# A perceiver layer on one core: opening zeros over all rows, the value bias in one product, output weights from slot 249, output projections four slots sooner, the last division behind the seam

## The reference, cut to what matters

```python
# cross-attention on the context, keys and queries rms-normed, masked by length
qh = rms_norm(q @ Wq, q_norm_w); kh = rms_norm(kv @ Wk, k_norm_w); vh = kv @ Wv
o = softmax(where(mask, qh @ kh.T / 8, NEG_INF)) @ vh
x = x + o @ Wo
# causal self-attention over 128 rows, with biases
qkv = einsum('bsd,dthe->bsthe', x, w_qkv) + b_qkv
x = x + einsum('bqhe,hed->bqd', softmax(q @ k.T / 8 - 1e9 * (1 - causal)) @ v, w_out) + b_out
# feed-forward, activations and weights rounded to fixed steps
x = x + act_qdq(act_qdq(gate * sig) * up) @ lpbq_dequant(w_down).T
```

## Time and profile before

| | |
|---|---|
| median of 3 runs | 1226.51 us |
| profiled execution, its time | 1228.04 us |
| its span | 1226.1 us |
| TensorE busy | 1161.4 us (95%) |
| VectorE | 814.8 us (66%) |
| ScalarE | 735.0 us (60%) |
| GpSimd | 874.3 us (71%) |
| transfers | 209.98 MB, queue q1 84.4% of 16 engines' span |
| cross-attention ends | about 967 us |
| self-attention | 971 to 1092 us |
| feed-forward | 1093 to 1226 us |

### The profile page before, as it was taken

One profiled execution on the slowest core, in us unless ns is written; L12 is line 12 of the kernel. 1 busy time (PEld: TensorE's weight loads), 2 busy tenths in 40 slices (PEclk: granted clock), 3 DMA queues, 4 the chain that ended last, 5 costly groups with the idle time before them and its releaser, 6 DMA issues. The chain is left out here.

```text
span 1226.1 us, 31362 instructions
## 1 busy us (share of the span) xinstructions
PE 1161.4 (95%) x11841; PEld 876.1 (71%) x11845; DVE 814.8 (66%) x1780; ACT 735.0 (60%) x1329; POOL 874.3 (71%) x750
## 2 busy tenths in 40 slices
PE   6899999999999999999999999999998899979958
PEld 4677777877888888788888878788885667534423
DVE  5778777697766678676666877666655444542772
ACT  5366655775767667666666776667666336512760
POOL 2689999888888898788888888898887423510510
PEclk9999999999999999999999999999999999989979
DMA  6579999999999999999999998999999533972000
GB/s 208 147 136 187 210 179 192 187 227 207 185 208 193 199 189 217 236 178 202 199 189 203 215 206 178 198 182 216 191 161 238 152 88 70 236 163 39 1 1 35
DMA packets 562345, 209.98 MB, mean 171 GB/s; under 512 B 506770, under 2 KB 529298, under 8 KB 562196
## 3 DMA queue, kind: packets, MB, share of 16 engines
q1 hardware_dynamic: 562196, 207.98, 84.4%
HBM read 66.27 MB, written 23.07 MB: 73 GB/s over the span
## 5 line engine op out<-in xcount | busy, mean ns | idle before, releaser
L144 PE MATMUL pair<-arena 128*128 128x256 f16 x2048 | 559.8, 273 | 15.6 <-DVE arena L655 7.8
L146 PE MATMUL pair<-arena 128*128 128x256 f16 x2048 | 558.9, 273 | 0.0
L145 PE MATMUL pair<-arena 128*128 128x256 f16 x2048 | 558.8, 273 | 0.0
L513 POOL TENSOR_TENSOR p_parts<-probs,p_parts 128x512 f16<-128x512 f32 x256 | 307.7, 1208 | 19.8 <-ACT p_parts L620 19.4
L523 POOL TENSOR_TENSOR k_rinv<-k_ms,half_neg 128x8 f32<-128x8 f32 x128 | 226.3, 1768 | 103.4 <-DVE k_ms L718 102.6
L144 PEld LDWEIGHTS pair<-arena 128*128 128x128 f16 x2048 | 200.2, 98 | 90.7 <-issue 47.7
L703 DVE CUSTOM_DVE_ANT_0 probs<-bank,mask 128x512 f32<-128x512 f32 x256 | 175.1, 684 | 114.8 <-PE bank L868 110.1
L620 ACT ACTIVATE p_parts<-probs 128x512 f16<-128x512 f32 x256 | 160.9, 629 | 100.7 <-DMA pt<-p_parts 89.2
L146 PEld LDWEIGHTS pair<-arena 128*128 128x128 f16 x2048 | 200.4, 98 | 23.7
L145 PEld LDWEIGHTS pair<-arena 128*128 128x128 f16 x2048 | 200.4, 98 | 20.8
L597 ACT ACTIVATE probs<-probs,neg_max 128x512 f32<-128x512 f32 x256 | 182.9, 714 | 8.7 <-DVE neg_max L712 8.7
(11 more groups left out here) (276 smaller groups left out, 1878.0 us busy)
## 6 DMA issues: line engine op xcount, KB each, us to landing
raws<-in_ctx_t_dram SPq DMA_DIRECT2D x64, 256.0 KB, 3.3
side_kept<-side_parts SPq DMA_DIRECT2D x40, 256.0 KB, 3.7
arena<-side_kept SPq DMA_DIRECT2D x40, 256.0 KB, 4.5
w_kept<-ffn_turned SPq DMA_DIRECT2D x36, 256.0 KB, 3.4
side_raw<-in_w_qkv_dram SPq DMA_DIRECT2D x24, 256.0 KB, 3.3
arena<-w_kept SPq DMA_DIRECT2D x24, 256.0 KB, 4.0
pt<-p_parts SPq DMA_TRANSPOSE x240, 3.7
ffn_raw<-in_w_gate_dram SPq DMA_DIRECT2D x12, 256.0 KB, 3.6
```

The costliest lines, as they stand in the source:

```text
L144: nc.tensor.matmul(to, x_hi[k], w_hi[k], start=(k == 0), stop=False)
L145: nc.tensor.matmul(to, x_hi[k], w_lo[k], start=False, stop=False)
L146: mm = nc.tensor.matmul(to, x_lo[k], w_hi[k], start=False, stop=(k == n - 1))
L513: nc.gpsimd.tensor_tensor(p_parts[n % PTS][:, 1, :], probs[n % PROBS][:, :], p_parts[n % PTS][:, 0, :], ALU.subtract).then_inc(p_lo_done, 1)
```

## The change

- `zeros` has 128 rows, and the opening product of a unit uses all of them.
- `OUT_FIRST, NORM_AT, WO_FIRST = (258, 262, 266), (262, 266), 249`: output projections and norms stand four slots sooner, and the two idle products of L876 stay in slot 257 alone. LAST is 274.
- The eight pieces of `Wo` are loaded one a slot from slot 249, each behind a wait for the projection that last reads its place in `ctx_lo`; the layout of `wo_at` changes so that a piece covers just two context tiles. The other 24 pieces keep two a slot, from slot 256.
- The last unit's division, split and transpose leave cross-attention and stand at the head of self-attention's lists. The second product of the ring (bank 7) waits for the division.
- The values' bias: one tile `bv_parts` holds the high part in all rows and the low part in rows 32 to 63; the weights `two_rows` are 1 in rows 0 and 32, zero elsewhere. One product of 128 rows takes the place of two of one row.

```diff
-OUT_FIRST, NORM_AT = (262, 266, 270), (266, 270)
+OUT_FIRST, NORM_AT, WO_FIRST = (258, 262, 266), (262, 266), 249
...
-        wo_at = arena[:, 24576:32768].rearrange("p (a k n) -> p a k n", a=2, k=GROUPS)
+        wo_at = arena[:, 24576:32768].rearrange("p (k a n) -> p a k n", a=2, k=GROUPS)
...
-        zeros = sb("zeros", [1, 2 * VW], F16, c)
+        zeros = sb("zeros", [P, 2 * VW], F16, c)
...
-        LAST = PARTS + PV_LAG + 4
+        LAST = PARTS + PV_LAG
...
-            return n // 8 if n is not None and n % 8 == 7 else None
+            return n // 8 if n is not None and n % 8 == 7 and n < PARTS - 1 else None
...
+                if 0 <= (j := slot - WO_FIRST) < GROUPS:
+                    if j == 0:
+                        for i in range(2):
+                            sp.wait_ge(side_kept_done[i], 16 * SIDES // 2)
+                    sp.wait_ge(proj_done, PARTS - GROUPS + 1 + j)
+                    sp.dma_start(side_home(j), side_kept[j].rearrange("p (a n) -> p a n", a=2)).then_inc(side_in[j // 4], 16)
                 if slot == PARTS:
                     sp.wait_ge(proj_done, PARTS)
...
-                for j in range(2 * (slot - PARTS), 2 * (slot - PARTS) + 2):
-                    if 0 <= j < DRAINED:
+                for j in range(GROUPS + 2 * (slot - PARTS), GROUPS + 2 * (slot - PARTS) + 2):
+                    if GROUPS <= j < DRAINED:
...
-                        nc.tensor.matmul(bank[7][:, 0:2 * VW], zeros[0:1, 0:P], zeros[0:1, :], start=True, stop=False)
+                        nc.tensor.matmul(bank[7][:, 0:2 * VW], zeros[:, 0:P], zeros[:, :], start=True, stop=False)
...
-                sp.dma_start(bv_row[i], g["b_qkv"][2 * E + D * i:2 * E + D * (i + 1)].partition_broadcast(1)).then_inc(bv_in, 16)
+                sp.dma_start(bv_row[i], g["b_qkv"][2 * E + D * i:2 * E + D * (i + 1)].partition_broadcast(P)).then_inc(bv_in, 16)
...
+            sp.wait_ge(last_lo_done, 1)
+            sp.dma_start_transpose(ot[:, B - 1, :, GROUPS - 1, :], last_parts[:, :, :].rearrange("p a n -> p (a n)")).then_inc(ot_in[1], 16)
             x_turned(0)
...
-            nc.gpsimd.memset(ones[:, :], 1.0).then_inc(ready, 1)
+            nc.gpsimd.memset(two_rows[:, :], 0.0).then_inc(zeroed, 1)
...
+            for i in range(2):
+                pool.wait_ge(zeroed, 3 + i)
+                nc.gpsimd.affine_select(out=two_rows[:, :], in_=two_rows[:, :], compare_op=ALU.not_equal, fill=1.0, base=-32 * i,
+                                        pattern=[[0, P]], channel_multiplier=1).then_inc(zeroed, 1)
...
+            pool.wait_ge(last_hi_done, 1)
+            nc.gpsimd.tensor_tensor(last_parts[:, 1, :], last_o[:, :, :].rearrange("p h e -> p (h e)"), last_parts[:, 0, :],
+                                    ALU.subtract).then_inc(last_lo_done, 1)
...
             def placed(key):
+                if at[key] == 1:
+                    pe.wait_ge(last_o_done, 1)
...
-                nc.tensor.matmul(to[:, :], ones[0:1, :], bv_hi[0:1, n * D:(n + 1) * D], start=True, stop=False)
-                nc.tensor.matmul(to[:, :], ones[0:1, :], bv_lo[0:1, n * D:(n + 1) * D], start=False, stop=False)
+                nc.tensor.matmul(to[:, :], two_rows[:, :], bv_parts[:, n * D:(n + 1) * D], start=True, stop=False)
...
+            nc.vector.reciprocal(last_rec[:, :], last_new[:, :, HD]).then_inc(last_rec_done, 1)
+            dve.wait_ge(last_rec_done, 1)
+            nc.vector.tensor_tensor(last_o[:, :, :], last_new[:, :, 0:HD], last_rec[:, :].unsqueeze(2).to_broadcast([P, 2, HD]),
+                                    ALU.mult).then_inc(last_o_done, 1)
```

More of the change, by code:

```diff
@@ L129, in program @@
             o_parts = [sb(f"o_parts{i}", [P, 2, P], F16, attn) for i in range(2)]
+            o_rec = [sb(f"o_rec{i}", [P, 2], F32, attn) for i in range(2)]
+            o_n = [sb(f"o_n{i}", [P, 2, HD], F32, attn) for i in range(2)]
             row_parts = [sb(f"row_parts{i}", [P, 2, D], F16, attn) for i in range(2)]
@@ L157, in cross_attention @@
             g[n] for n in ("resid", "ot", "xt", "wo_at", "w_qkv_at", "side_kept", "side_in", "ot_in", "xt_in", "o_parts", "bqk"))
-        o_rec = [sb(f"o_rec{i}", [P, 2], F32, c) for i in range(2)]
-        o_n = [sb(f"o_n{i}", [P, 2, HD], F32, c) for i in range(2)]
+        o_rec, o_n = g["o_rec"], g["o_n"]
         side_raw = [sb(f"side_raw{i}", [P, D], F32, c) for i in range(2)]
@@ L679, in _ @@
                 d = slot // 2 - 1
-                if (n := part(PV_LAG + 1, slot)) is not None and n % 8 == 7:
+                if (n := part(PV_LAG + 1, slot)) is not None and n % 8 == 7 and n < PARTS - 1:
                     u = n // 8
@@ L897, in _ @@
                     if first == 0:
-                        pe.wait_ge(k_n_done, PROJS)
-                        pe.wait_ge(v_lo_done, PROJS)
+                        pe.wait_ge(k_n_done, PROJS - (b < 2))
+                        pe.wait_ge(v_lo_done, PROJS - (b < 2))
                         for i in range(2):
@@ L919, in self_attention @@
         HALF, TURNED = 2 * P, 11
+        last_o, last_rec, last_parts = g["o_n"][1], g["o_rec"][1], g["o_parts"][1]
+        last_new = bank[7][:, 0:2 * VW].rearrange("p (h v) -> p h v", h=2)
         NORMS = [("out", 2), ("out", 3)] + [("again", b) for b in range(B)]
@@ L942, in self_attention @@
         less, beyond = sb("less", [P, P], BF16, c), sb("beyond", [P, 4, P], BF16, c)
-        ones = sb("ones", [P, P], F16, c)
-        bv_row = [t[0:1, :, :].rearrange("p h e -> p (h e)") for t in o_n]
-        bv_hi, bv_lo = (sb(n, [P, E], F16, c) for n in ("bv_hi", "bv_lo"))
+        two_rows = sb("two_rows", [P, P], F16, c)
+        bv_row = [t[:, :, :].rearrange("p h e -> p (h e)") for t in o_n]
+        bv_parts = sb("bv_parts", [P, E], F16, c)
         b_out = sb("b_out_rows", [P, D], F32, c)
@@ L1253, in o_high @@
                                      ACT.Copy).then_inc(oh_done, 1)
-            act.wait_ge(ready, 5)
+            act.wait_ge(last_o_done, 1)
+            act.wait_ge(ot_in[1], 16 * (B * GROUPS // 2 - 1))
+            nc.scalar.activation(last_parts[:, 0, :], last_o[:, :, :].rearrange("p h e -> p (h e)"), ACT.Copy).then_inc(last_hi_done, 1)
             for i in range(16):
@@ L1262, in _ @@
                     for h in range(2):
-                        nc.scalar.activation(bv_hi[0:1, D * h:D * (h + 1)], bv_row[h], ACT.Copy, scale=W2_UP).then_inc(bv_hi_done, 1)
+                        nc.scalar.activation(bv_parts[:, D * h:D * (h + 1)], bv_row[h], ACT.Copy, scale=W2_UP).then_inc(bv_hi_done, 1)
                 if i == 10:
                     x_high(1)
+            act.wait_ge(ready, 4)
             high_v(0, 0)
```

12 lines of the change are left out of this document (6 added, 6 removed).

## The result

The changed kernel took 1218.39 us (median of 6 runs, 1213.48 to 1221.33) beside 1232.3 us for the kernel before: a ratio of 0.9906, 95% interval 0.9885 to 0.9928, or 11.5 us less. The forecast was 12.9 us less, more than the kernel gives: what is left lies just inside one per cent. The time of 1218.39 us is at the upper end of the range, partly because the kernel before itself came out at 1232.3 us here and at 1226.51 us in the runs shown.

A forecast was written before the change was run, and what follows sets the result against it. TensorE was taken to bound the kernel from 60 to 930 us, busy 856.0 of 870 us. Terms -5.8 - 1.4 - 3.7 + 0.3 - 2.3 = -12.9 us from the 1226.51 us median gave 1213.7 us, range 1210 to 1218.5.

The forecast's parts named there:

- Zeros, -5.8 us: Opening product of each cross-attention unit: row-count changes cost 0.195 us, saved in 30 units; bounds 0 and -6.3.
- the rival by which the wide product costs as much as the narrow one: Opening zeros: first term 0, bias saves only 0.9 us, kernel at 1219.9 us; chance 10%.
- Bias, -1.4 us: Self-attention value bias: four of eight merged products count, 0.35 us each; bounds -0.7 and -3.1.
- Projections, -3.7 us: End of cross-attention: output projections four slots sooner, TensorE's end at 963.0 us against 966.67.
- Loads, +0.3 us: Output-weight loads from slot 249: Sync queue issues the transpose of probabilities later, 0 to 1.3 us late.
- the second rival: Moved loads and thinner slack: late transposes in slots 253 to 257, single-part chain in 270 to 273; +2 to +4; 19%.
- Seam, -2.3 us: Between attention stages: last division moved behind, TensorE arrives last and stands 2.0 us instead of 4.33.
- Clock, 0: Behind the seam: same clock loss after 2.0 us idle; -1.2 if it stays up, +0.5 if as long as at 1075.
- The sum: Whole kernel: -5.8 - 1.4 - 3.7 + 0.3 - 2.3 = -12.9 us, giving 1213.7 us.

The follow-up runs named there:

- a_fill: a_late plus six idle products of 512 columns ahead of TensorE's wait for the third batch's heads in self-attention; ratio 0.9887 to the kernel before.
- a_late: Changed kernel, first output projection waiting for only four weight pieces, self-attention weight loads begun in slot 258 instead of 256; 1216.75 us, ratio 0.9879 to the kernel before.
- after: The changed kernel with the whole change, against the kernel before; 1218.39 us, ratio 0.9906.
- after_again: The changed kernel once more, unaltered, in a second comparison against the kernel before; ratio 0.9932.
- a_div_back: Changed kernel with the last head's division and splitting back in cross-attention; ratio 0.9953 to the kernel before.
- a_bias_back: Changed kernel with the value bias back to two products of one row; ratio 0.9930 to the kernel before.
- a_zeros_back: Changed kernel with the opening zeros back to a product of one row; ratio 0.9952 to the kernel before.
- b_bias: Kernel before with only the value bias changed, one product of 128 rows instead of two of one row; ratio 0.9990.

## Why the prediction was right and wrong

- **Zeros, -5.8 us.** The spacing was right to 0.01 us (0.20 for 0.195 forecast), and the rival by which the wide product costs as much as the narrow one fell. The trace agrees with the Trainium skill's "TensorEngine Tiling (Array Packing)", section "Key Properties", that a change of tiling mode drains the array: about 0.1 us on either side of the product here. The step that was too large is the multiplication by 30: it took every 0.1 us on TensorE as 0.1 us of the kernel. Stretch A is 3.1 us shorter in the mean (6.2 in the profiled pair), the timed runs say 4.7. Of the missing 2.7 us, 1.3 to 2.1 are idle times that grow, in good part waits for transposes; the rest is not assigned. The prediction read the 14 us of not being busy in the earlier trace rows as mostly spacing between products; 12.3 of them are idle times of 0.3 us and more. That reading is what made every 0.1 us look like a gain.
- **Bias, -1.4 us.** The size was right, 1.5 us, and the reason was not: luck. The step counted four of the eight products. All eight gain, and two waits that were not foreseen, 0.9 us for ScalarE's exponentials and 0.5 us for VectorE, take about half of it back. Its second effect was not foreseen either: the wait ahead of the third projection shrank from 2.15 to 1.77 us (2.4 and 2.0 us in the means of four executions and of nine; a_fill, whose idle products fill it, is not among them), and the clock stayed up there, 1.7 us in this pair of executions.
- **Projections, -3.7 us.** The slot by slot working was right for TensorE's own work: once the transfers are out of the way (a_late, a_fill), B is 30.17 us, and with the shorter last product (0.20 for 0.38) that is 3.4 us less than before. In the changed kernel B was 31.2 to 35.6 us, 33.0 in the mean of five executions (after, after_again, a_div_back, a_bias_back, a_zeros_back). So about 0.5 us were gained on before's 33.37, or 1.2 on the mean of the four kernels with the old slots (34.0, b_bias among them).
- **Loads, +0.3 us: the step that failed.** It asked when the transposes behind the loads are issued, and took the landing of the key transpose to stay as it was. It did not ask when the loads themselves land: the eighth piece, issued in slot 256, is wanted by the first projection in slot 258, since that waits for all eight. That cost 0.9 to 2.5 us, and from 2.36 us on the low clock as well. And the sentence on the key transpose ("moves by 0.5 us and is needed 5.5 us later") was small for the issue, which moved by 0.6 to 1.4 us against the drain's opening product, and left out the landing, which went from 3.5 us to 5.6 to 7.0. Together the term was near +3 instead of +0.3 (B of 33.0 for 30.2 once both waits are gone): the second rival's size (+2 to +4), but with other victims, the output weights and the key transpose in slots 258 and 261, not transposes of probabilities in 253 to 257. In the 12 us ahead of the drain's opening product, where it looked for them, only 0.24, 0.41 and 0.55 us of such waits stood, in three executions.
- **Seam, -2.3 us.** -2.7, idle 1.58 or 1.59 us for 4.33 in each of seven executions (C is 2.9 us shorter, since the last product is too). TensorE came last there, as the step said, and the distance from the last arrival was 0.4 us shorter than in the kernel before.
- **Clock, 0.** At the seam it stayed at 1.00 in six of those seven executions and fell in one. Full clock is worth 1.3 us there against the 2.6 us at 0.50 in the kernel before, so this belonged into the sum and not among the bounds. The step that took the same loss after 2.0 us of idle time was wrong.
- **The sum.** The errors ran both ways: about +2.7 from the zeros, +2.2 to +2.9 from the loads and the drain, -0.4 at the seam, -1.3 from its clock, -0.1 from the bias, and up to -1.7 where the clock also stays up at the third projection. They leave -9 to -11.5 us, where the two comparisons have 11.5 and 8.4. That the total comes this near to 12.9 is in part luck: gains that the sum had at nothing or too small, the clock's above all, made up for a third or more of what zeros and loads lost. This sum of means is worked out after the fact and is no finer than 2 us.
- **Why one profiled pair shows 14.4 us.** That execution had the shorter wait for the pieces and the clock up at all three places; the second one, with 1218.9 us of span, was 2.2 us longer up to the second opening product, 0.8 in A, 2.0 in B and 1.0 in D. Stretch A varies by 4 us between executions of nearly the same code, and goes with the idle times of 0.3 us and more in it (10.8 us where A was 813.2, 14.2 us where it was 817.4); why these differ stays open.

## What to carry to other kernels

A load that is moved forward has three dates to check, not one: its own landing against its first user, the landing (not the issue) of every transfer that it now shares the engines with, and the semaphore by which its user waits, which may ask for more than is needed. Give a wait only the pieces that the next instructions read, and put bulk loads behind the last transfer that somebody is short of: that made the same reordering worth 3.4 us of the drain instead of about one. And a gain that repeats in every unit is to be multiplied only by the units in which nothing else is near: sum the idle times that end in a transfer before trusting the product.

## What the runs showed of the hardware

- A product of one row of 130 columns among products of 128 rows costs 0.20 us more than one of 128 rows: units without waits take 27.57 us in the four traces with the first and 27.36 to 27.37 in the ten with the second. Idle rows of zeros are cheaper here than a change of shape.
- A key transpose of 128 by 1024 f16 elements landed in 3.5 (twice), 3.8, 5.0 and 6.4 us where four loads of 256 KB and one write of that size had been issued in the 5 us ahead of it, and in 5.6 to 7.0 (seven executions) where it was five loads and the write in 4 us. With one load and the write in the 4 us ahead of it, it was 4.5 and 4.7. So the number of loads alone does not give the landing, and no run tells what else does.
- At the places followed here (drain, seam, third output projection) the granted clock fell to 0.50 (1.2 GHz) behind, or up to 1.4 us after, idle times of 4.53, 4.33 (three executions), 3.86, 3.04, 3.02, 2.71, 2.60, 2.56, 2.50, 2.40, 2.36, 2.31, 2.15 and 2.04 us, and stayed at 1.00 behind 2.23, 1.92, 1.87, 1.86, 1.82, 1.77 (twice), 1.75, 1.73, 1.66, 1.59 (in the drain), 0.89 and 0.67 us and, at the seam, six times of seven behind 1.58 or 1.59. The length of the idle time thus goes with the fall but does not decide it alone. Once down it stayed so for 2.6 to 5.8 us of full work: behind the same seam with the same idle time (4.33 us) for 2.6 in before and 5.8 in b_bias. From there to the last product ahead of the values' bias it took 27.3 and 28.8 us in the two, and 26.0 where the clock stayed at 1.00. The 1.5 us between the first two are a difference from run to run by the clock alone.
